# Attention and post-norm on eight cores: projection steps moved ahead of the last P·V matmuls, and a LayerNorm kept on one engine

## What is computed

```python
# attention with its own pre-norm and residual
h = layernorm(x) * ln_gamma + ln_beta
q, k, v = split(h @ w_qkv + b_qkv)            # 16 heads of 64
attn = softmax(q @ k.T / 8) ; out = (attn @ v) @ w_out + b_out
x = layernorm(x + (x + out))
# feed-forward on 64 channels
s = x @ Win + bin_
h = relu(s[..., None] * W1 + b1)
g = einsum('btmh,mh->btm', h, W2) + b2
x = layernorm(x + (g @ Wout + bout))
```

## Time and profile before

| | before |
|---|---|
| median of 2 runs | 2031.65 us (2031.0 to 2032.3) |
| profiled execution | 2033.93 us |
| its span, first to last instruction, slowest core | 2032.4 us (cores 2018.8 to 2032.4) |
| part two, 229 to 1690 us: PE, ACT, DVE busy | 1195, 1146, 355 us of 1461 |
| part three, 1729 to 2032 us: PE, DVE, ACT busy | 138, 151, 76 us of 303 |

### The profile page before, as it was taken

The page is one execution under the profiler, slowest core; times in us unless marked ns, Lnnn a source line. Parts: engine busy times, 40 slices in busy tenths (PEclk is TensorE's granted clock), DMA queues, the critical chain, the costliest instruction groups (busy, mean ns, idle before and its releaser), DMA issues. The chain is left out here.

```text
span 2032.4 us, 26688 instructions; the slowest of 8 cores (2018.8 to 2032.4 us)
## 1 busy us (share of the span) xinstructions
PE 1429.1 (70%) x8552; PEld 505.5 (25%) x8552; DVE 629.6 (31%) x870; ACT 1285.4 (63%) x1262; POOL 26.1 (1%) x35
## 2 busy tenths in 40 slices
PE   1544699688869977986898799789866772546343
PEld 0222233223323322332232233223222220212111
DVE  3664222322231232223222212322231001453554
ACT  1432487677868777876878687788768881222222
POOL 0000000000000000000000000000000000000000
PEclk9766699999999999999999999999999996767665
DMA  6331000100100010001001000100000005102202
GB/s 101 106 106 48 1 6 1 11 1 6 11 1 6 1 11 1 6 1 11 1 6 11 1 6 1 11 1 6 1 1 1 1 1 94 42 0 83 83 0 83
DMA packets 44596, 44.34 MB, mean 22 GB/s; under 512 B 34993, under 2 KB 35122, under 8 KB 44466
## 3 DMA queue, kind: packets, MB, share of 16 engines
q1 hardware_dynamic: 16162, 33.72, 5.6%
q0 software_dynamic: 28304, 8.92, 4.3%
HBM read 43.16 MB, written 8.39 MB: 25 GB/s over the span
## 5 line engine op out<-in xcount | busy, mean ns | idle before, releaser
L847 ACT ACTIVATE PT_sb<-score_ps,negB_sb 128x1024 bf16<-128x1024 f32 x1024 | 1140.9, 1114 | 305.5 <-PE score_ps L764 228.0
L762 PE MATMUL score_ps<-qT_sb,kT_sb 64*128 64x512 bf16 x1024 | 394.8, 391 | 195.2 <-ACT PT_sb L847 99.1
L778 PE MATMUL pv_ps<-PT_sb,v_sb 128*64 128x512 bf16 x1024 | 406.0, 396 | 27.5 <-ACT PT_sb L847 18.0
L782 PE MATMUL pv_ps<-PT_sb,v_sb 128*64 128x512 bf16 x1024 | 407.0, 397 | 0.0
L764 PE MATMUL score_ps<-qT_sb,kT_sb 64*128 64x512 bf16 x1024 | 398.8, 395 | 0.0
L788 PE MATMUL z_ps<-PT_sb,onesb_sb 128*64 128x512 bf16 x1024 | 394.4, 385 | 0.0
L785 PE MATMUL z_ps<-PT_sb,onesb_sb 128*64 128x512 bf16 x1024 | 394.4, 385 | 0.0
L617 PE MATMUL qkv_ps<-xhq_sb,wq_sb 128*128 128x512 bf16 x1120 | 295.2, 389 | 13.2 <-DVE kT_sb L632 7.9
L762 PEld LDWEIGHTS score_ps<-qT_sb,kT_sb 64*128 64x128 bf16 x1024 | 92.7, 93 | 572.9 <-issue 572.0
L778 PEld LDWEIGHTS pv_ps<-PT_sb,v_sb 128*64 128x64 bf16 x1024 | 111.7, 109 | 208.5 <-issue 158.3
L802 DVE RECIPROCAL zb_sb<-z_ps 128x512 f32<-128x512 f32 x32 | 107.4, 3358 | 165.6 <-PE z_ps L788 125.9
(11 more groups left out here) (84 smaller groups left out, 834.8 us busy)
## 6 DMA issues: line engine op xcount, KB each, us to landing
xtile_sb<-x SPq DMA_DIRECT2D x32, 512.0 KB, 4.1
xres_sb<-x SPq DMA_DIRECT2D x16, 512.0 KB, 8.4
out<-u_sb SPq DMA_DIRECT2D x16, 512.0 KB, 3.6
wq_sb<-wqkv POOLq DMA_DIRECT2D x24, 256.0 KB, 5.0
wout_sb<-wout POOLq DMA_DIRECT2D x1, 2048.0 KB, 23.0
win_sb<-win POOLq DMA_DIRECT2D x1, 128.0 KB, 23.0
rw_sb<-rw POOLq DMA_DIRECT2D x1, 128.0 KB, 22.8
w2b_sb<-w2b POOLq DMA_DIRECT2D x1, 128.0 KB, 22.9
```

The lines of the kernel that those rows point to most:

```text
L762: e.matmul(o, w, r, start=True, stop=True))
L778: a=s0, b=s1: e.matmul(o, w, r, start=a, stop=b, skip_group_check=True))
L782: e.matmul(o, w, r, start=a, stop=b, skip_group_check=True))
L847: e.activation(out=o, in_=i_, func=AF.Exp, bias=b, scale=0.125))
```

## The change

It does two things. In `finish_qt` the three generator steps are taken first, ahead of PE's wait for the last exponential and the 8 pv and z matmuls of key tiles 30 and 31. In `batched_ln` all four tiles are normalised on DVE, as the even ones were; ACT keeps only the conversion to bfloat16. The small tile `nm_sb`, its guard, and the wait of L1028 for ACT's reading of `u_sb` are gone.

```diff
     def finish_qt(h, pqt, hit):
-        sc.wait("tensor", ss, h["exp_done"][NKT - 1])
-        for j in (NKT - 2, NKT - 1):
-            h["pvz_done"][j] = emit_pvz(pqt, j, hit, h["exp_done"])
         if gen is not None:
             next(gen, None)
             next(gen, None)
             next(gen, None)
+        sc.wait("tensor", ss, h["exp_done"][NKT - 1])
+        for j in (NKT - 2, NKT - 1):
+            h["pvz_done"][j] = emit_pvz(pqt, j, hit, h["exp_done"])
         zbh = zb_sb[:]
...
         for t in range(4):
             u_ap = u_sb[:, (uslot0 + t) * C:(uslot0 + t + 1) * C]
-            if outs2[t] is not None and t % 2 == 1:
-                nm = nm_sb[:, slot * 4 + t:slot * 4 + t + 1]
-                sc.wait("vector", ss, nmg.get((slot, t), 0))
-                v_nm = sc.v(lambda e, o=nm, i_=mv[:, t * 2:t * 2 + 1],
-                            r=rst[:, t:t + 1]:
-                            e.tensor_scalar(o, i_, r, -1.0,
-                                            op0=AluOpType.mult,
-                                            op1=AluOpType.mult))
-                sc.wait("scalar", sv, v_nm)
-                sc.s(lambda e, o=outs[t], i_=u_ap, r=rst[:, t:t + 1], b=nm:
-                     e.activation(out=o, in_=i_, func=AF.Identity,
-                                  scale=r, bias=b))
-                s_c = sc.s(lambda e, o=outs2[t], i_=outs[t]:
-                           e.copy(out=o, in_=i_))
-                nmg[(slot, t)] = s_c
-                rets.append(("s", s_c))
-                continue
             v_ap = sc.v(lambda e, o=outs[t], i_=u_ap, m=mv[:, t * 2:t * 2 + 1],
...
                 sc.wait("vector", st, t_op)
-                sc.wait("vector", ss, u_sc_rd.get(tt, 0))
```

More of the change, by code:

```diff
@@ L268, in build_nc @@
                 mv2_sb=SB34("mv2_sb", [128, 16], F32),
-                nm_sb=SB34("nm_sb", [128, 8], F32),
                 rstd2_sb=SB34("rstd2_sb", [128, 8], F32),
@@ L863, in p34 @@
     stats2_sb, mv2_sb, rstd2_sb = L["stats2_sb"], L["mv2_sb"], L["rstd2_sb"]
-    nm_sb = L["nm_sb"]
     A_ps, B_ps, C_ps, F_ps = L["A_ps"], L["B_ps"], L["C_ps"], L["F_ps"]
@@ L935, in batched_ln @@
         sc.wait("vector", ss, s_r)
-        nmg = L.setdefault("nm_guard", {})
         rets = []
@@ L983, in p34 @@
     x2cast_st = [[0] * 4, [0] * 4]
-    u_sc_rd = {}
     def p3a_stage(sl):
@@ L1038, in p3bc_stage @@
             x2cast_st[spar] = [c for (k, c) in ln_rets]
-            for t, (k, c) in enumerate(ln_rets):
-                if t % 2 == 1:
-                    u_sc_rd[t] = c
             for tt in range(4):
```

## The result

The changed kernel takes 2042.6 us (median of 35 runs; before 2033.2, median of 34). The ratio is 1.0042, with a 95% interval of 1.0033 to 1.0050: 8.5 us slower, within 2% and clear of the noise. The medians count every run; in some executions the cores of one die or of both ran at a lower granted clock and the kernel took up to 6% longer, and the ratios, and the reading of `e1_ln_only` on its cores 4 to 7 alone, leave that out. Against the 2031.65 us shown ahead of the prediction that is 2040.2 us, where the forecast said 2032.

What follows compares the result with a forecast made beforehand. No engine was full: ACT set the pace or waited for scores from PE. Terms of +7.0, +8.3, -6.0, +1.5 and -10.6 us summed to +0.2 us on 2031.65, say 2032 us, range 2022 to 2042.

Steps and rivals of the forecast that it cites:

- The move fills no hole: In `finish_qt`, PE does not idle at the last exponential's wait, so two blocks only swap; the 3.26 us stop stays.
- Boundary one: First `finish_qt` boundary in a subgroup: reciprocal 1.25 us later, 1.0 us lost each, +7.0 us over seven (4.3 to 7.6).
- the term for the clock: One more fall of the TensorE clock, behind boundary two's longer hole: +1.5 us, ends -1.5 and +4.
- rival two: The clock falls at boundaries one and two in every subgroup, 1.5 us per fall: 2045 us; chance 0.12.
- Boundary two: Second boundary: reciprocal 1.19 us later in a closed chain, ACT's stop grows equally, +8.3 us over seven (7 to 9).
- Boundary three: Third boundary: the early L617 block removes a 0.75 us wait, chain gains 0.85 us, -6.0 us over seven (-6.6 to -4).
- The LayerNorm: Part three: ACT loses two L950 per slice, 2.66 us each slice, -10.6 us in four slices (ends -10.6 and -6).
- Rival three: Part three: the LayerNorm change gives nothing because DVE becomes late; 2042.6 us, chance 0.05.
- Rival one: Boundary one absorbs the reciprocal's delay and the clock stays as it is: -8.3 us, 2023 us; chance 0.13.
- The sum: Whole kernel: part two +10.8 us, part three -10.6 us, together +0.2 us, say 2032 us; chance 0.70.
- The sign of idle time before the exponentials: In the changed kernel's profile, the exponentials' idle time was to be up by about 11 us.
- The ends of the terms: Whole kernel: the four terms' ends were said to give about -8 to +9 us, 2024 to 2041 us.

Runs made afterwards that it cites:

- e1_ln_only: The changed kernel with `finish_qt` put back, leaving the LayerNorm change alone; ratio 0.9937 to the kernel before, 12.8 us faster.
- e3_move_b1: The kernel before with the generator steps first at boundary one only, LayerNorm as before; in one execution tile 1 takes 308.1 us, +8.4.
- e6_fill_b1: The changed kernel plus 18 unread transposes on PE in the new wait ahead of tile 1's first pv matmul; ratio 0.9978, median 2028.8 us.
- e5_b3_ln: The changed kernel with the generator steps first at boundary three only, LayerNorm change kept; ratio 0.9902, median 2016.8 us.
- e8_fill_b2: The kernel of `e5_b3_ln` plus 64 unread transposes on PE in the 3.96 us hole of boundary two; ratio 0.9841, median 2003.0 us.

## Why the prediction was right and wrong

*The move fills no hole.* Right, and seen directly: ACT's stop before the exponential of key tile 1 is 3.26 us in both kernels at boundary one.

*Boundary one, +7.0 us (4.3 to 7.6).* The delay was right in each link: reciprocal 1.24 us late (1.25 forecast), pv matmul with a new wait of 1.00 us ("near 1 us"), and 0.94 us of cost per tile where the clock holds (1.0 forecast), as `e3_move_b1` and `e6_fill_b1` show. But the tile took +14.7 us. What failed is the term for the clock: I put it at boundary two only, and gave the fall at boundary one to rival two with 0.12, on the ground that PE has holes of 1.07 us there now without a fall. In the changed kernel it falls there in six subgroups of seven on the slowest core (five to seven, by core), and costs about 1.54 us each time (2.48 - 0.94), the 1.5 of rival two. Over the seven that is 8.2 us that the forecast had at nothing, beside 6.5 for the delay. So on boundary one rival two was right, in place and in price.

*Boundary two, +8.3 us and +1.5 for the clock.* The chain was exact: 5.15 us against 3.96, 5.16 against 3.97. Together +9.8 forecast and +10.3 measured. The ground for the +1.5, that one hole in seven went without a fall, was a misreading: the lower level follows all seven holes before as well. What grew is the time spent there in tile 2, from 31 to 37 us per core to 37 to 41. That the sum came out all the same was luck.

*Boundary three, -6.0 us.* Right: -6.5 in the changed kernel, 5.9 where the clock stays up, and `e5_b3_ln` turned it into a faster kernel.

*The LayerNorm, -10.6 us.* Right, within what the end of the kernel varies by: the last part is 11.3 us shorter in the changed kernel and 8.8 in `e1_ln_only` (before, it differs by up to 8 us between cores), alone the change gives 12.8 us with an interval that holds 10.6, and each of the four slices is 2.66 us shorter from its first conversion to the first copy out of `B_ps` on the slowest cores (7.19 before, 4.53 after). Rival three falls: on the slowest core the four conversions run back to back in all four slices, and before the second LayerNorm's normalisations that follow such a slice DVE still waits 3.1 to 3.3 us for ACT, where some 3 were forecast. Rival one falls as well: of 1.24 us of delay only 0.3 us were absorbed (0.94 us of cost).

*The sum.* Forecast +0.2, measured +8.5 us. Taking boundary one at 14.7 and not 7.0 gives +7.9. The sign of idle time before the exponentials told the same: it was to grow by about 11 us and grew by 22.1. The range of 2022 to 2042 held 2040.2 near its upper end, which lies toward rival two. The ends of the terms as they stand add up to -7.4 and +10.6, not to -8 and +9, which moves the range little. The rule that I cited from the Trainium skill ("TensorE: Matmul & The Clock Gate", Part 1, What's actually happening), that a throttled clock is the default and activity releases it, spoke for this side. By that rule the trace agrees: the added activity of `e6_fill_b1` and `e8_fill_b2` held the granted clock at 1.00 and took 8.2 us off tile 1 and 9.5 us off tile 2. I had weighed the rule at boundary two alone.

Open is why the clock falls at boundary one in five to seven subgroups of seven in the changed kernel and in one to three with the same wait in `e3_move_b1`, by core. The wait alone doesn't decide it; no run here tells what else does.

## What to carry to other kernels

When independent work is moved ahead of a block, ask first whether the engine waited at that point; if it did not, the move only swaps which of two releases comes late, and one looks for who waits for the block that moved back. An edit over several places of one loop should be tried place by place: here one of three was worth 6 us, and the other two cost 25. And a wait of one microsecond on TensorE can cost two and a half, so its price has to be read with the clock of the stretch behind it, not from its length.

## What was not expected of the hardware

Work that nobody reads made the kernel faster. 18 transposes of 128 columns in a 1.0 us wait, seven times, brought tile 1 from 314.4 to 306.2 us; 64 in a 3.96 us wait brought tile 2 from 323.0 to 313.5; the granted clock in these stretches went from 0.79 and 0.5 to 1.00. A hole as short as 1.00 us, behind a PE wait of 0.90 us for the exponential that the kernel before has too, was followed by the lower clock level in six of seven subgroups on the slowest core; in `e3_move_b1`, with the same two waits, in one to three.

The eighth subgroup has the same instructions in both kernels and took 161.6 us before and 162.6 after. Its tiles are 39.2, 40.0, 41.5 and 41.1 us before and 39.8, 41.0, 41.0 and 40.7 after on the slowest cores. By the clock's records it spends 13.6 us at the lower level in both, on the slowest core before in its last two tiles and after in all four. Whether that makes the one microsecond is not shown.
